# Attention and mixture-of-experts block on one core: the router's small tables first, gate bias rows ahead of the table matmuls, one up bias load sooner

## The chip, the cores and the metric

The kernel runs on 1 core of one Trainium2 chip. The metric is the device time of one execution in microseconds (us), the median over several runs. Lower is better.

## The reference

The input x is [1, 64, 32, 256]. The layer is an axial attention with a pair bias, added to x, and after it a mixture of experts over 2048 tokens of width 256, added again. What matters here is the second half:

```python
logits = x @ router_w + router_b                 # 2048 x 8
probs = jax.nn.softmax(logits, axis=-1)
top_v, top_i = jax.lax.top_k(probs, TOP_K)       # TOP_K = 2
top_v = top_v / jnp.sum(top_v, axis=-1, keepdims=True)
weights = jnp.zeros((T, E)).at[jnp.arange(T)[:, None], top_i].set(top_v)
gate = jnp.einsum('td,edi->eti', x, gate_w) + gate_b[:, None, :]
up = jnp.einsum('td,edi->eti', x, up_w) + up_b[:, None, :]
h = jax.nn.silu(gate) * up
expert_out = jnp.einsum('eti,eid->etd', h, down_w) + down_b[:, None, :]
y = jnp.einsum('te,etd->td', weights, expert_out)
```

There x is the normalised token, and all of it is float32. There are 8 experts with 512 hidden columns each.

## The kernel before

**Stages.** The kernel first normalises x and stacks it by token. Then a loop of 8 steps does the attention of 32 columns each; beside it the weights of one expert per step are loaded and split into a float16 high and low part (ScalarE and GpSimd). Then comes the router, and then 39 blocks of 128 token slots, each belonging to one expert: gather the tokens from DRAM, gate and up matmul, silu, product, down matmul, scale, and add into the output with an indirect DMA. The order of work on every engine is written out by hand, and semaphores tie the engines together. Each of them runs its own list strictly in order, so a waiting instruction holds back all that stands behind it.

**The router.** Of the names in the views, att_t, kq, z_two, gate, w_stage and att_n are buffers of the attention that the router uses again. Its steps:

- GpSimd makes thirteen tables. Three of them are large or belong to the output: `r_number` (L489, an iota of 128x1024), its float16 copy `r_count` (L490), and zeros in `ws_flat` (L492), which two DMAs (L494) write to the output's pad rows. These are 256 rows behind the 2048 real ones, into which empty slots scatter. The other ten are small (L497 to L508): `before`, the triangle for counting tokens; iotas for tiles, thresholds, token numbers and experts (`r_rev`); and masks. Every table increments route_p. The order of GpSimd's list is: last weight split (L467), the large iota and copy, zeros and pad DMAs, the ten small tables, four normalised tiles of tokens (L513), then the second half of the softmax (L517 to L526).
- VectorE takes the statistics of all tokens (L1426, L1429), their reciprocal roots (L1201 to L1204, behind a square root of ScalarE) and the negated mean (L1432), which releases rs_ready. Then it waits for all thirteen tables, copies `r_rev` to float32 (L1436), and goes on from the logits (L1442) through the two largest of eight, the mark of both, the running count (L1458), slots (L1465 to L1484), and `r_values` and `r_place` (L1487 to L1498). `r_count` is read there for the first time. At L1508 it makes the gather indices.
- ScalarE copies transposed tokens, normalises twelve tiles (L1098) after rs_ready, takes one exponential (L1115), and then copies the gate bias of each expert from PSUM to SBUF (L1123), after the output rows of `x_rows` have been stored.
- TensorE transposes the logits (L810), spreads each expert's gate bias row over 128 partitions (L818, `gate_bias_rows`: one matmul with 8 partitions for one expert, shown as two in the trace), does the counting matmuls (L824 to L826), 32 matmuls that put token numbers into slots (L833, "table matmuls"), and warming matmuls (L571, `keep_warm`) that compute nothing needed. `GATE_BANK` says which of the eight PSUM banks takes which expert's bias row; the seventh and eighth row (e of 6 or more) reuse banks 0 and 1 and wait until ScalarE has emptied them.
- SyncE issues the transfers: token rows to DRAM in four DMAs (`token_rows`, L368), then the routing weights next to them (L373), whose elements are 32 bytes. GpSimd's first gather (L541) waits for all of these, for the pads, for the output rows, and for L1508.

**Loads in the attention loop.** SyncE's list is, for each step j, the value placement of step j+1 (L338, four DMAs), a copy of tokens (L326), and the three weight loads of expert j+1 (L309). In `load_weights` four loads of the up bias are slipped in (`spread_up_biases`, L292), 512 KB each over 128 partitions. They go into the stacked tokens, and therefore wait until the token copies have landed (z_in0, z_in1). Three stand in the loads of the seventh expert (e is 6) and the fourth behind the gate load of the eighth.

```python
                    if e == EXPERTS - 2 or (e == EXPERTS - 1 and k == 0):
                        for i in range(2):
                            sp.wait_ge(s[f"z_in{i}"], 16 * (PAIRS // 2 - 1))
                        spread_up_biases(k if e == EXPERTS - 2 else 3)
```

Of the kernel before, what the change touches and what calls it, by code (L numbers as in the profile page):

```python
# [7 lines left out]
L_COL = 256  # L8
# [3 lines left out]
EXPERTS = 8  # L12
FF = 512
P = 128
# [13 lines left out]
TOKENS = D_MODEL * N_SEQ  # L28
TILES = TOKENS // P
TOP_K = 2  # L30
SLOT = P
# [8 lines left out]
PIECE = ASSIGN // PIECES  # L40
GATE_BANK = (0, 1, 2, 5, 6, 7, 0, 1)
# [6 lines left out]
def build(nc, x, pairs, ln_m_g, ln_m_b, ln_p_g, ln_p_b, Wq, Wk, Wv, Wg, bg, Wb, Wo, bo,  # L48
# [5 lines left out]
    with ctx:  # L54
# [48 lines left out]
        bank = [banks[:, i, :] for i in range(8)]  # L103
# [45 lines left out]
        N_TABLES = 13  # L149
        N_CONST, N_PAR, N_CENTER, N_ONES, N_PREP = 10, 18, 7, 3, 1 + 1 + 1 + 1 + 2  # L150
# [57 lines left out]
        rev_f = att_t[:, 328:336]  # L208
# [61 lines left out]
        def _(sp):  # L270
# [28 lines left out]
            def load_weights(e):  # L299

                parts = (gate_w[e].rearrange("(c p) i -> p c i", p=P), up_w[e].rearrange("(c p) i -> p c i", p=P),
                         down_w[e].rearrange("(c p) l -> p c l", p=P))
                for k in range(3):
                    if e >= 1:
                        if k < 2:
                            sp.wait_ge(s["w_hi_done"], 2 * (e - 1) + k + 1)
                        sp.wait_ge(s["w_lo_done"], 3 * (e - 1) + k + 1)
                    c = 2 if k < 2 else 4
                    sp.dma_start(w_stage[:, k, :].rearrange("p (c i) -> p c i", c=c),  # L309
                                 parts[k]).then_inc(s[f"w_in{k}"], 16)  # L310
                    if e == EXPERTS - 3 and k >= 1:
                        sp.wait_ge(s["x1_ready"], 1 + PAIRS // 2)
                        rows_to_out(0, k - 1)
                    if e == EXPERTS - 2 or (e == EXPERTS - 1 and k == 0):
                        for i in range(2):
                            sp.wait_ge(s[f"z_in{i}"], 16 * (PAIRS // 2 - 1))
                        spread_up_biases(k if e == EXPERTS - 2 else 3)
# [74 lines left out]
        def _(pool):  # L392
# [91 lines left out]
            def table(ins):  # L484
                ins.then_inc(s["route_p"], 1)
                n_r[0] += 1
                pool.wait_ge(s["route_p"], n_r[0])
            pool.wait_ge(s["w_lo_done"], 3 * EXPERTS)
            table(pool.iota(r_number, pattern=[[1, P], [0, PIECE]], base=0, channel_multiplier=0))  # L489
            table(pool.tensor_copy(r_count, r_number))  # L490
            pool.wait_ge(s["x1_ready"], 1 + PAIRS)
            table(pool.memset(ws_flat[:, 0:L_COL], 0.0))  # L492
            for i in range(2):
                pool.dma_start(out[TOKENS + SLOT * i:TOKENS + SLOT * (i + 1), :], ws_flat[:, 0:L_COL])\  # L494
                    .then_inc(s[f"y_landed{i}"], 16)

# [12 lines left out]
            assert n_r[0] == N_TABLES  # L509

            pool.wait_ge(s["rs_ready"], 1)
            for n in range(TILES - 4, TILES):
                pool.tensor_scalar(xn[:, n, :], x_rows[:, n, :], mv[:, n, 0:1], rs_col[:, n:n + 1],  # L513
                                   ALU.subtract, ALU.mult).then_inc(s["xn_pool"], 1)

# [50 lines left out]
        def _(pe):  # L566
# [255 lines left out]
            gate_bias_rows(range(3))  # L822
# [5 lines left out]
            gate_bias_rows(range(3, 6))  # L828
# [7 lines left out]
            gate_bias_rows(range(6, EXPERTS))  # L836
            keep_warm(3, bank[3])
# [352 lines left out]
        def _(dve):  # L1190
# [239 lines left out]
            dve.wait_ge(s["mean_ready"], 2 * TILES)  # L1430
            rsqrt(4, rs_col, mv[:, :, 1], EPS_TOK, sd_col, tmp_col, None)
            dve.scalar_tensor_tensor(out=neg_mean, in0=mv[:, :, 0], scalar=-1.0, in1=rs_col,  # L1432
                                     op0=ALU.mult, op1=ALU.mult).then_inc(s["rs_ready"], 1)

            dve.wait_ge(s["route_p"], N_TABLES)
            step(dve.tensor_copy(rev_f, r_rev))  # L1436
# [49 lines left out]
            values = r_values.rearrange("p t (c a) -> p t c a", c=PIECES)  # L1486
            step(dve.tensor_tensor(values, r_count[:, 0:BLOCKS, :].unsqueeze(2).broadcast_to(by_block),  # L1487
# [164 lines left out]
```

## Time and profile before

| what | value |
|---|---|
| median of 3 runs | 350.35 us |
| lowest and highest | 348.79 and 351.41 us |
| the profiled execution's own time | 347.03 us |
| its span | 345.2 us |
| TensorE, VectorE, ScalarE, GpSimd busy | 283.2, 273.9, 195.2, 209.1 us |
| mean granted TensorE clock | 0.926 |

The profile is of one execution. Its span is what the profiler saw between first and last instruction. Shares of busy time are averages over stages: TensorE's 82% of the span is 100% in the blocks and far less in the router. A row of a timeline has start, duration, engine, line, operation and, in brackets, the idle time before it with what ended it. PE is TensorE, DVE VectorE, ACT ScalarE, POOL GpSimd, SP SyncE; an engine's name with q is its instruction queue. The granted clock is 1.00 at 2.4 GHz and 0.50 at 1.2 GHz.

### The profile page before, as it was taken

What the parts mean: (1) busy time and instruction counts of PE and PEld (TensorE: products, weight loads), DVE (VectorE), ACT (ScalarE), POOL (GpSimd) and SP (SyncE); (2) the same over time, 40 slices, a digit from 0 to 9 for tenths busy, and PEclk for the clock granted to TensorE, in tenths of its full rate; (3) what the DMA queues carried; (4) which work ended last, traced back from release to release, by engine and by line L of the source; (5) the groups of instructions that cost most, each with busy time, mean ns of one, the idle gap of its engine ahead of it and who ended that gap; (6) DMA issues with size and microseconds to landing.
All of it is one profiled execution on the core that took longest, in us unless ns stands there. A gap on an engine that the chain in (4) does not pass through costs nothing.

```text
span 345.2 us, 11090 instructions
## 1 busy us (share of the span) xinstructions
PE 283.2 (82%) x3762; PEld 176.0 (51%) x3763; DVE 273.9 (79%) x568; ACT 195.2 (57%) x357; POOL 209.1 (61%) x171
## 2 busy tenths in 40 slices
PE   0496857868877768918989999999999999999970
PEld 0186434535554446404346666666666666666640
DVE  3998786979999998879578888778787888888840
ACT  0268676958779756494245555555555555555430
POOL 2633042777888987861523666685848676776461
PEclk9998995899999987955599999999999999999996
DMA  7550111455868999646235977877777786977552
GB/s 181 96 173 14 64 36 29 133 193 158 238 223 234 279 313 329 171 102 148 70 76 77 142 125 122 144 129 123 125 128 130 124 141 118 144 134 122 94 78 30
DMA packets 72288, 47.36 MB, mean 137 GB/s; under 512 B 48536, under 2 KB 63896, under 8 KB 72128
## 3 DMA queue, kind: packets, MB, share of 16 engines
q1 hardware_dynamic: 63904, 36.19, 41.5%
q0 software_dynamic: 7584, 10.65, 20.1%
q8 instruction: 15, 0.25, 0.3%
q10 hardware_dynamic: 768, 0.14, 0.3%
q14 instruction: 17, 0.14, 0.2%
HBM read 23.43 MB, written 9.63 MB: 96 GB/s over the span
## 4 chain that ended last, share of the span: by engine, by line
PE 44%; DVE 18%; issue 12%; DMA 10%; POOL 7%; ACT 5%; POOLq 2%; ACTq 0%; DVEq 0%; SPq 0%
PE bank L871 22%; PE bank L894 10%; DMA out_dram<-z_two,gate 7%; DVE maxes L1333 4%; DVE s_exp L1342 3%; PE bank L607 2%; DVE e_t L1352 2%; PE bank L859 2%; POOL w_exp L456 2%; PE bank L571 2%; DMA w_stage<-in_L_ffn_up_w_dram 2%; ACT kq L1044 2%; DMA w_exp<-in_L_conv_pairs_dram 2%; PE bank L698 1%; POOLq L548 1%
## 5 line engine op out<-in xcount | busy, mean ns | idle before, releaser
L871 PE MATMUL bank<-w_exp,v_t 128*128 x468 | 114.1, 381 | 1.6 <-DVE v_t L1534 1.6
L553 POOL DMA_INDIRECT out_dram<-z_two,gate x39 | 67.4, 1729 | 50.3 <-ACT z_two L1167 27.6
L871 PEld LDWEIGHTS bank<-w_exp,v_t 128*128 128x128 f16 x468 | 45.9, 98 | 41.9 <-issue 3.9
L894 PE MATMUL bank<-w_exp,kq 128*128 x468 | 57.7, 273 | 0.8 <-DVE w_stage L1580 0.8
L541 POOL DMA_INDIRECT w_stage<-token_rows,gate x39 | 41.1, 1053 | 22.3 <-issue 7.9
L894 PEld LDWEIGHTS bank<-w_exp,kq 128*128 128x128 f16 x468 | 45.5, 98 | 14.8 <-issue 1.3
L1158 ACT ACTIVATE kq<-w_stage 128x512 f16<-128x512 f32 x38 | 23.9, 630 | 38.0 <-DVE w_stage L1563 38.0
L456 POOL TENSOR_TENSOR w_exp<-w_stage,w_exp 128x1024 f16<-128x1024 f32 x16 | 34.2, 2136 | 18.0 <-ACT w_exp L1055 18.0
L1570 DVE TENSOR_TENSOR kq<-w_stage,kq 128x512 f16<-128x512 f32 x38 | 26.3, 692 | 16.7 <-ACT kq L1158 16.7
L1555 DVE TENSOR_TENSOR kq<-bank,z_stack 128x512 f32<-128x512 f32 x39 | 27.0, 691 | 7.9 <-PE bank L871 7.8
L1563 DVE TENSOR_TENSOR w_stage<-s_exp,kq 128x512 f32<-128x512 f32 x39 | 27.2, 697 | 4.7 <-DVE kq L1555 1.8
L1131 ACT ACTIVATE v_t<-bank 128x256 f16<-128x256 f32 x39 | 14.9, 382 | 22.7 <-PE bank L859 22.1
L1144 ACT ACTIVATE s_exp<-s_exp 128x512 f32<-128x512 f32 x39 | 24.5, 628 | 5.3 <-DVE s_exp L1550 5.0
L1550 DVE TENSOR_TENSOR s_exp<-bank,x_rows 128x512 f32<-128x512 f32 x39 | 26.6, 683 | 0.0
L1352 DVE STREAM_TRANSPOSE e_t<-s_exp 128x1024 f32<-128x1024 f32 x16 | 19.8, 1240 | 4.5 <-ACT s_exp L1050 4.5
L1044 ACT ACTIVATE kq<-bank,kb_head,head_mask 128x512 f32<-128x512 f32 x32 | 22.2, 781 | 0.0
L1333 DVE TENSOR_REDUCE maxes<-bank 128x32 f32<-128x1024 f32 x16 | 19.5, 1216 | 3.3 <-PE bank L698 3.3
L1167 ACT ACTIVATE z_two<-w_stage,gate 128x256 f32<-128x256 f32 x39 | 19.3, 494 | 4.9 <-DMA out_dram<-z_two,gate 3.7
L1050 ACT ACTIVATE s_exp<-s_exp 128x1024 f32<-128x1024 f32 x16 | 16.9, 1055 | 8.4 <-DVE s_exp L1342 8.2
L571 PE MATMUL bank<-ones_h,ident_h 128*128 128x512 f16 x29 | 10.2, 513 | 13.4 <-DVE small L1204 13.4
L1342 DVE TENSOR_TENSOR s_exp<-bank,maxes 128x1024 f32<-128x1024 f32 x16 | 19.3, 1204 | 0.3
L1534 DVE TENSOR_TENSOR v_t<-bank,v_t 128x256 f16<-128x256 f32 x39 | 16.2, 415 | 3.7 <-ACT v_t L1131 3.7
(251 smaller groups left out, 493.0 us busy)
## 6 DMA issues: line engine op xcount, KB each, us to landing
w_stage<-in_L_ffn_gate_w_dram SPq DMA_DIRECT2D x8, 512.0 KB, 3.9
w_stage<-in_L_ffn_up_w_dram SPq DMA_DIRECT2D x8, 512.0 KB, 4.9
w_stage<-in_L_ffn_down_w_dram SPq DMA_DIRECT2D x8, 512.0 KB
v_t<-v_row SPq DMA_DIRECT2D x32, 72.0 KB, 2.3
x_rows<-in_x_dram SPq DMA_DIRECT2D x8, 256.0 KB, 6.3
out_dram<-x_rows SPq DMA_DIRECT2D x4, 512.0 KB, 6.0
z_stack<-in_L_ffn_up_b_dram SPq DMA_DIRECT2D x4, 512.0 KB, 7.1
token_rows<-v_t SPq DMA_DIRECT2D x4, 512.0 KB, 6.1
```

What stands on the lines that cost most here:

```text
L456: pool.tensor_tensor(lo, w_stage[:, k, :], hi, ALU.subtract).then_inc(s["w_lo_done"], 1)
L541: pool.indirect_dma_start(xg[b % 4], None, token_rows, bass.IndirectOffsetOnAxis(t_gather[:, b:b + 1], 0))\
L553: pool.indirect_dma_start(out, bass.IndirectOffsetOnAxis(t_scatter[:, b:b + 1], 0), yw[b % 2], None, compute_op=ALU.add).then_inc(s[f"y_la ...
L871: mm = pe.matmul(GU[par][k][:], xs[par][:, c, :], w_exp[:, w * W_EXP + k * W_PIECE + c * FF:][:, bass.ds(e, FF)], start=(n == 0), stop=(n ...
L894: mm = pe.matmul(YB[:, 0:L_COL], hs[par][:, c, :], w_exp[:, w * W_EXP + 2 * W_PIECE + c * L_COL:][:, bass.ds(e, L_COL)], start=(n == 0), s ...
L1044: act.activation(k_exp[:, h, :], bank[5 if j else 1], ACT.Identity, bias=kb_head[:, h:h + 1], scale=head_mask[:, h:h + 1]).then_inc(s["k_r ...
L1333: dve.tensor_reduce(maxes[:, c, :], banks[:, 2 * c:2 * c + 2, :].rearrange("p g (a m) -> p (g a) m", m=N_SEQ), AX.X, ALU.max).then_inc(s[" ...
L1342: dve.tensor_tensor(s_exp[:, c, :, :].rearrange(rows, m=N_SEQ), banks[:, 2 * c:2 * c + 2, :].rearrange(rows, m=N_SEQ), maxes[:, c, :].unsq ...
L1352: dve.transpose(e_t[:, c, :, :].rearrange("p g t -> p (g t)"), s_exp[:, c, :, :].rearrange("p g t -> p (g t)")).then_inc(s["et_ready"], 1)
L1550: dve.tensor_tensor(g_sum[par], bank[2 * par][:], gate_b_all[:, bass.ds(e * FF, FF)], ALU.add)\
L1555: dve.tensor_tensor(u_sum[par], bank[2 * par + 1][:], up_b_all[:, bass.ds(e * FF, FF)], ALU.add)\
L1563: dve.tensor_tensor(h_sb[par], g_silu[par], u_sum[par], ALU.mult).then_inc(s["h_ready"], 1)
```

## The change

It moves instructions and changes no arithmetic.

- GpSimd: the ten small tables come first, then the large iota and its copy, then the four normalised tiles, and the zeros with the two pad DMAs last. VectorE waits for the ten (`N_SMALL`) before its copy of `r_rev`, and that copy moves ahead of the reciprocal roots; for the large table it waits where it first reads it.
- TensorE: five gate bias rows instead of three ahead of the counting matmuls, the other three behind those and ahead of the table matmuls, none behind the table matmuls. There, seven warming matmuls instead of three. Experts 4 and 5 exchange their banks 6 and 7.
- SyncE: the fourth up bias load moves from behind the gate load of the eighth expert to behind that of the sixth (e is 5).

```diff
-GATE_BANK = (0, 1, 2, 5, 6, 7, 0, 1)
+GATE_BANK = (0, 1, 2, 5, 7, 6, 0, 1)
...
+        N_SMALL = N_TABLES - 3
...
-                    if e == EXPERTS - 2 or (e == EXPERTS - 1 and k == 0):
+                    if e == EXPERTS - 2 or (e == EXPERTS - 3 and k == 0):
...
             pool.wait_ge(s["w_lo_done"], 3 * EXPERTS)
-            table(pool.iota(r_number, pattern=[[1, P], [0, PIECE]], base=0, channel_multiplier=0))
-            table(pool.tensor_copy(r_count, r_number))
             pool.wait_ge(s["x1_ready"], 1 + PAIRS)
-            table(pool.memset(ws_flat[:, 0:L_COL], 0.0))
-            for i in range(2):
-                pool.dma_start(out[TOKENS + SLOT * i:TOKENS + SLOT * (i + 1), :], ws_flat[:, 0:L_COL])\
-                    .then_inc(s[f"y_landed{i}"], 16)
-
             table(pool.memset(before, 0.0))
...
             table(pool.memset(r_one8, 1.0))
-            assert n_r[0] == N_TABLES
-
+            assert n_r[0] == N_SMALL
+            table(pool.iota(r_number, pattern=[[1, P], [0, PIECE]], base=0, channel_multiplier=0))
+            table(pool.tensor_copy(r_count, r_number))
             pool.wait_ge(s["rs_ready"], 1)
             for n in range(TILES - 4, TILES):
                 pool.tensor_scalar(xn[:, n, :], x_rows[:, n, :], mv[:, n, 0:1], rs_col[:, n:n + 1],
                                    ALU.subtract, ALU.mult).then_inc(s["xn_pool"], 1)
+
+            table(pool.memset(ws_flat[:, 0:L_COL], 0.0))
+            assert n_r[0] == N_TABLES
+            for i in range(2):
+                pool.dma_start(out[TOKENS + SLOT * i:TOKENS + SLOT * (i + 1), :], ws_flat[:, 0:L_COL])\
+                    .then_inc(s[f"y_landed{i}"], 16)
...
-            gate_bias_rows(range(3))
+            gate_bias_rows(range(5))
             pe.wait_ge(s["sel_ready"], 1)
...
-            gate_bias_rows(range(3, 6))
+            gate_bias_rows(range(5, EXPERTS))
             pe.wait_ge(s["values_ready"], 1)
...
-            gate_bias_rows(range(6, EXPERTS))
-            keep_warm(3, bank[3])
+            keep_warm(7, bank[3])
...
             dve.wait_ge(s["mean_ready"], 2 * TILES)
+            dve.wait_ge(s["route_p"], N_SMALL)
+            step(dve.tensor_copy(rev_f, r_rev))
             rsqrt(4, rs_col, mv[:, :, 1], EPS_TOK, sd_col, tmp_col, None)
...
-
-            dve.wait_ge(s["route_p"], N_TABLES)
-            step(dve.tensor_copy(rev_f, r_rev))
...
+            dve.wait_ge(s["route_p"], N_SMALL + 2)
             step(dve.tensor_tensor(values, r_count[:, 0:BLOCKS, :].unsqueeze(2).broadcast_to(by_block),
```

GpSimd behind the last weight split, before: w_stage holds first the large table (L489, L490), then the zeros (L492).

```order
L489 IOTA w_stage 128x1024
L490 CAST w_stage<-w_stage 128x1024
L492 MEMSET w_stage 128x256
L494 DMA out_dram<-w_stage 128x256 x2
L497 MEMSET z_two 128x128
L498 AFFINE_SELECT z_two<-z_two 128x128
L500 IOTA att_t 128x128
L501 IOTA att_t 128x16
L503 IOTA att_t 64x16 x2
L505 IOTA att_t 128x8
L506 MEMSET kq 128x128
L507 MEMSET kq 128x8
```

And now, from the last of the small tables' iotas on (the tables from the memset of z_two to this iota stand ahead of it, right behind the weight split):

```order
L499 IOTA att_t 128x8
L500 MEMSET kq 128x128
L501 MEMSET kq 128x8
L502 MEMSET kq 128x8
L504 IOTA w_stage 128x1024
L505 CAST w_stage<-w_stage 128x1024
L508 TENSOR_SCALAR v_t<-x_rows,small 128x256 x4
L511 MEMSET w_stage 128x256
L514 DMA out_dram<-w_stage 128x256 x2
L518 TENSOR_SCALAR kq<-kq 128x16
```

The large table went behind the small ones, and the zeros and pad DMAs behind the normalised tiles (L508), right ahead of the softmax denominator (L518).

VectorE at the token statistics, before: the cast to att_t is the copy of r_rev, and the instruction behind it makes the logits.

```order
L1429 BN_AGGR small<-g_pre 128x2 x16
L1201 RECIPROCAL small<-small 128x16
L1202 SCALAR_TENSOR_TENSOR small<-small 128x16
L1203 SCALAR_TENSOR_TENSOR small<-small 128x16
L1204 SCALAR_TENSOR_TENSOR small<-small 128x16
L1432 SCALAR_TENSOR_TENSOR g_pre<-small 128x16
L1436 CAST att_t<-att_t 128x8
L1442 TENSOR_TENSOR att_n<-bank,small 128x128
```

And now:

```order
L1429 BN_AGGR small<-g_pre 128x2 x16
L1432 CAST att_t<-att_t 128x8
L1201 RECIPROCAL small<-small 128x16
L1202 SCALAR_TENSOR_TENSOR small<-small 128x16
L1203 SCALAR_TENSOR_TENSOR small<-small 128x16
L1204 SCALAR_TENSOR_TENSOR small<-small 128x16
L1434 SCALAR_TENSOR_TENSOR g_pre<-small 128x16
L1441 TENSOR_TENSOR att_n<-bank,small 128x128
```

The cast and its wait went ahead of the reciprocal.

TensorE from the transposed logits to the warming matmuls, before; v_row holds the gate bias rows:

```order
L810 MATMUL bank<-ident,v_t 128x128 x4
L818 MATMUL bank<-v_row,ident 128x512 x3
L824 MATMUL bank<-kq,ones_h 128x8
L825 MATMUL bank<-kq,z_two 128x128
L826 MATMUL bank<-kq,ones_h 128x128
L818 MATMUL bank<-v_row,ident 128x512 x3
L833 MATMUL bank<-gate,s_exp 128x39 x32
L818 MATMUL bank<-v_row,ident 128x512 x2
L571 MATMUL bank<-ones_h,ident_h 128x512 x3
```

And now:

```order
L811 MATMUL bank<-ident,v_t 128x128 x4
L819 MATMUL bank<-v_row,ident 128x512 x5
L825 MATMUL bank<-kq,ones_h 128x8
L826 MATMUL bank<-kq,z_two 128x128
L827 MATMUL bank<-kq,ones_h 128x128
L819 MATMUL bank<-v_row,ident 128x512 x3
L834 MATMUL bank<-gate,s_exp 128x39 x32
L572 MATMUL bank<-ones_h,ident_h 128x512 x7
```

Two bias rows went from behind the table matmuls to ahead of the counting matmuls, and the three behind the counts are now experts 5, 6 and 7.

## Rows read from the trace of the kernel before

**Rows 1.** Windows: length, busy us (instructions) of PE, PEld, DVE, ACT, POOL; PEclk, DMA share, GB/s.

```profile
148.00:170.00 22.00, 14.71 (x52) 6.53 (x52) 19.23 (x59) 11.85 (x22) 10.75 (x13) 0.50 0.48 117
170.00:178.00 8.00, 6.49 (x29) 3.07 (x29) 4.25 (x8) 2.93 (x8) 2.82 (x3) 0.91 0.27 65
178.00:288.00 110.00, 110.00 (x692) 69.09 (x693) 89.56 (x161) 59.07 (x134) 70.02 (x50) 1.00 0.76 124
```

**Rows 2.** Chain that ended last, 140 to 172 us: start us, us, what.

```profile
140.73 1.41 POOL w_stage L489
...
147.68 0.11 POOL kq L508
...
161.04 2.49 PE bank L833 x32
163.53 3.71 PE bank L818 x4
167.24 1.39 PE bank L571 x3
...
170.15 2.10 PE bank L871 x6
```

**Rows 3.** Timeline of VectorE, router stage: start us, us, then idle before and releaser.

```profile
145.01 0.25 DVE L1201 RECIPROCAL small<-small 128x16 f32<-128x16 f32 x1 [0.44 <-ACT small L1110]
...
145.93 0.17 DVE L1432 SCALAR_TENSOR_TENSOR g_pre<-small 128x16 f32<-128x16 f32 x1
147.81 0.17 DVE L1436 CAST att_t<-att_t 128x8 f32<-128x8 int32 x1 [1.71 <-POOL kq L508]
...
156.07 0.25 DVE L1476 RECIPROCAL kq<-kq 128x16 f32<-128x16 f32 x1
...
163.64 0.20 DVE L1508 TENSOR_SCALAR gate<-bank 128x39 int32<-128x39 f32 x1 [0.19 <-PE bank L833]
```

**Rows 4.** Timeline of GpSimd, router stage.

```profile
143.94 1.41 POOL L494 DMA_DIRECT2D out_dram<-w_stage  x2 [0.33 <-POOL w_stage L492]
...
147.90 4.90 POOL L513 TENSOR_SCALAR v_t<-x_rows,small 128x256 f32<-128x256 f32 x4
154.50 0.27 POOL L517 TENSOR_SCALAR kq<-kq 128x16 f32<-128x16 f32 x1 [1.71 <-ACT kq L1115]
...
164.74 1.11 POOL L541 DMA_INDIRECT w_stage<-token_rows,gate  x1 [6.38 <-DVE gate L1508]
```

**Rows 5.** SyncE's last small write to token_rows: its issue, and its time to landing.

```profile
159.00 1.08 SPq L373 DMA_DIRECT2D token_rows<-w_stage  x1
...
token_rows<-w_stage SPq DMA_DIRECT2D x1, 32.0 KB, 3.6
```

**Rows 6.** DMA queues, 154 to 158 us: packets, MB, share of 16 engines.

```profile
q1 hardware_dynamic: 1072, 1.06, 99.1%
```

**Rows 7.** Timeline of ScalarE, router stage.

```profile
152.16 1.28 ACT L1115 ACT_TABLE_LOAD   x1
154.20 0.22 ACT L1115 ACTIVATE kq<-kq 128x16 f32<-128x16 f32 x1 [0.76 <-DVE kq L1460]
...
155.84 2.04 ACT L1123 ACTIVATE x_rows<-bank 128x512 f32<-128x512 f32 x4
```

**Rows 8.** Timeline of TensorE, gate bias rows.

```profile
144.13 2.84 PE L818 MATMUL bank<-v_row,ident 8*128 8x512 f32 x6
...
154.51 5.48 PE L818 MATMUL bank<-v_row,ident 8*128 8x512 f32 x6
```

**Rows 9.** DMA queues, 145 to 147 us.

```profile
q0 software_dynamic: 96, 0.26, 37.2%
```

**Rows 10.** Value placement of the seventh step: last issue, its time to landing, its first reader.

```profile
116.00 0.59 SPq L338 DMA_DIRECT2D v_t<-v_row  x1
...
v_t<-v_row SPq DMA_DIRECT2D x1, 72.0 KB, 2.2
...
119.42 0.76 PE L714 MATMUL bank<-v_t,e_t 128*32 128x36 f32 x64 [0.25 <-DVE e_t L1352]
```

## The prediction

> **What bounds the kernel now.** I read the windows of busy time first, since they tell which stage has which limit. From 178 to 288 us TensorE is busy for 110.00 of 110.00 us at granted clock 1.00 [rows 1]: the expert blocks run at TensorE's pace, so whatever moves the first expert matmul moves the end by as much, and nothing in this change touches a block. Before it lies the router, and there the chain of waits is the view to follow. It runs on GpSimd through L489 (140.73) to L508, whose 0.11 us end at 147.79 [rows 2], and only then does VectorE go on: L1436 stands at 147.81 after 1.71 us of idle time put down to L508 [rows 3]. From there the chain is VectorE's small steps, then TensorE: 32 table matmuls from 161.04 to 163.53, four passes of gate bias rows (3.71 us), three warming matmuls (1.39 us) to 168.63, the first token transposes and, at 170.15, the first expert matmul [rows 2].
>
> The third view is what runs beside the chain. The gathers of token rows need the bookkeeping of L1508 (ends 163.84) [rows 3] and also the landing of everything written to token_rows; the first gather starts at 164.74 [rows 4], 0.90 after L1508. The last small write is issued at 159.00 and takes 3.6 us to land, 162.6 [rows 5]. So today that landing is 1.2 us early, but the DMA engines were 99.1% busy from 154 to 158 [rows 6].
>
> **The change, part by part.** The profiled execution took 347.03 us (span 345.2 and 1.8 around it). The runs' median is 350.35, 3.3 above; I work a difference on the former and subtract it from the latter.
>
> *GpSimd's order.* The ten small tables take 147.79 − 145.35 (end of the pad issues, 143.94 + 1.41 [rows 4]) = 2.44 us. Begun at 140.73 they end at 143.2. VectorE's aggregates end at 145.01 − 0.44 = 144.57 [rows 3], so its new wait for ten tables is already met by 1.4 us. Its moved cast (0.17 us) sits in the 0.44 us in which it waits for ScalarE's root anyway: cost nothing, and 0.2 if that root came sooner. The router's first multiply follows L1432 (ends 146.10) instead of L1436 (147.98): 1.71 of idle plus the cast and a handoff, **1.9 us** sooner on VectorE.
>
> The large iota and its cast now follow. Old GpSimd took from 140.73 to 143.94 for these two and the memset, so they are done by 143.2 + 3.2 = 146.4 at the latest, against 146.10 when L513 can start. L513 (4.90 us) began at 147.90 and now ends by 151.3 [rows 4]; the memset and two pad issues (1.41 and some 0.3 + 0.3) end at 153.3. What is queued behind them is L517, which VectorE's L1476 waits for. ScalarE's table load still ends at 152.16 + 1.28 = 153.44, since its twelve normalisations did not move, and the exponential (0.22) [rows 7] gives L517 its data at 153.7, just after GpSimd is free; L517 ends at 154.0. L1476 stood at 156.07, now 154.2. Cover 0.2 us: the two edits meet almost at once.
>
> The Trainium skill speaks against exactly this move. The two old pad issues took 1.41 us together while VectorE worked through its statistics [rows 4]. SBUF — State Buffer, section "SBUF: two separate sides", says that GpSimd cannot write a DMA's descriptors while VectorE holds the port pair that both share. By the row the sum keeps 1.4 us for the issues; by the rule they could stretch over VectorE's router steps, the last rival below.
>
> *Bias rows on TensorE.* Six passes took 2.84 us at the fast clock (0.47 each) and 5.48 us at the slow one (0.91) [rows 8]. Five experts are ten passes: 144.13 to 148.9, in time that was idle: the next rows began at 154.51 [rows 8], right behind the router's counts, now 152.6. Three experts then stand ahead of the table matmuls. The first takes until 154.5. The next needs a bank that ScalarE empties: exponential over at 153.7, then what took 154.42 to 155.84, then 0.51 a copy [rows 7], thus 155.6. Two experts at 1.82 each end at 159.2, and the table matmuls can start at 161.04 − 1.9 = 159.1. Cost 0.1, or nothing at the fast clock. This is the new tight spot.
>
> Behind the table matmuls (end 161.6) 3.71 us of bias rows are gone and four warming matmuls are added: 7 x 0.46 = 3.2, so TensorE is ready at 164.9 instead of 168.6. What is late next is the data.
>
> *The pads among the row writes.* Around 145–147 us the software queue used 37.2% of 2 us on sixteen engines [rows 9], 0.74 us of all of them, in a lull. Now it comes at about 153, in the 99.1% stretch. The small writes are issued 1.9 sooner but stand behind it all: they land between 162.6 − 1.9 = 160.7 (nothing delays them) and 162.6 + 0.74 = 163.3. I take 163.3, the row of a full stretch being the nearest. The gather then starts 0.9 later, at 164.2. From its start to arrival is at least its own 1.11 us and at most 168.6 − 164.74 = 3.9; I take 3.2, nearer to the 3.6 of a small write. Transposes at 167.4 instead of 168.6: **1.2 us** is what the path gets out of the 1.9 and 3.7.
>
> *The clock.* The granted clock was 0.50 from 148 to 170 and averaged 0.91 over 170–178 [rows 1], so 1.4 us of that were at 1.2 GHz: the first 1.3 us of expert matmuls, costing half, 0.65. Before them TensorE had worked with almost no gap since 161.04. Now it stops at 164.9 for 2.5 us. Seven warming matmuls without a break may raise the clock sooner (gain up to 0.65), the pause may make it rise later. I take 0.
>
> *The up bias load.* Moved to the sixth expert's load, it adds 512 KB at about 107.5 us and waits for a copy that has just been issued. The stretch of [rows 6] moved 1.06 MB in 4 us, so it costs at most 2.0 us of the DMA engines. First in line behind it are the value placements: the last was issued at 116.00, landed 2.2 later at 118.2, and is wanted by L714 at 119.42 [rows 10], 1.2 us of cover. Loss 0 to 0.8; I take 0, since weight loads come faster than that stretch. At the end of the loop the last up weights come sooner, but VectorE sets that stage: 0.
>
> Sum: −1.2. Profiled, 345.8; against the median, **349.1**.
>
> **The rivals.** *The row writes do not gate* (25%). If the pads slip in without delaying the small writes, the gather follows L1508: 162.85, data at 166.05, TensorE ready at 164.9. Gain 2.6, with the fast clock 3.2: 347.1 to 347.8, say 347.5. For it: the landing is 1.2 us early today. Against: 99.1%.
>
> *The clock stays low* (13%), which ends slower. The pause from 164.9 to 167.4 is where it happens. Its price is half of each microsecond that expert matmuls run at 1.2 GHz beyond today's 1.3; it decides from 3.7 us on, when 2.4 x 0.5 eats the 1.2. At 6.5 us it costs 2.6: 350.35 + 1.4 = 351.8. For it: 22 us at 0.50 in which TensorE was busy most of the time. Against: full-width warming matmuls are what stood before today's rise, and there are more of them.
>
> *The up bias load hurts attention* (12%). The placements land 0.8 after they are wanted, the step slips once: gain 0.4, 349.9.
>
> *GpSimd is late for L517, or the pads delay the row writes by more than their own 0.74* (8%). L1476, and the small writes after it, come 1 to 1.5 us later than in my sum: gain 0 to 0.2, 350.3. The Trainium skill's rule above would act here; its own measured stretch of a descriptor write, from 620 to 3100 ns, would put each issue near 3 us, and no row here shows such a one.
>
> **How the numbers follow.** My case has 42%, and 0.65 either way for the clock. A measurement of this kernel tells about 1%, 3.5 us, from no change. Nearly every case lies within that: faster by more needs the first rival with the fast clock and some luck of runs whose spread is 348.79 to 351.41. Faster 0.14, within 1% 0.80, slower 0.06. The range takes the first rival's best less part of that spread at one end (346.4) and the slower rival at the other (351.7).
>
> **What would show it.** VectorE's cast straight after the aggregates with no 1.71 us wait; its L1508 counterpart ending near 161.9; the pad issues after L513 and software-queue traffic near 153–155; the small writes landing at 163, the first gather at 164.2 rather than 162.85; TensorE idle before its transposes near 167.4; the first expert matmul near 168.9. Wrong, if TensorE arrives there last, if a table matmul waits for bias rows by more than 0.2, if L1476 waits, or if the blocks no longer keep 110 of 110 us busy.

## The result, and the profile after

The changed kernel took 350.69 us (median of 20 runs, 348.61 to 351.99) against 348.79 (20 runs, 347.28 to 351.87). The ratio is 1.0053 with a 95% interval of 1.0034 to 1.0072. It is slower, by some 1.9 us, where 1.2 us less was forecast. The size is within the predicted 1%, the sign is not. The 350.35 that the forecast of 349.1 was taken from was a median of 3 runs, 1.6 above that of these 20. So the two times are 1.6 apart, while the change that was forecast and the one that was measured are 3.1 apart. The profiled execution took 351.16 us (span 349.3).

The windows of busy time, columns as in [rows 1]:

```profile
148.00:170.00 22.00, 18.23 (x58) 7.10 (x56) 19.28 (x64) 13.11 (x25) 10.42 (x15) 0.52 0.49 115
170.00:178.00 8.00, 6.76 (x22) 3.00 (x23) 1.88 (x5) 1.71 (x5) 4.20 (x5) 0.61 0.31 82
178.00:288.00 110.00, 108.59 (x677) 67.38 (x676) 89.57 (x160) 58.01 (x133) 66.72 (x50) 1.00 0.71 122
```

The last row still shows expert blocks at TensorE's pace. The middle row is the news: the granted clock over 170 to 178 us is 0.61, where it was 0.91. The two rows are not of the same work, though: before, the first expert matmul stood at 170.15, right at the window's start, and now it stands at 172.78.

The chain that ended last (start us, us, what):

```profile
117.41 0.59 SPq L339
118.05 3.10 DMA v_t<-v_row
121.19 0.77 PE bank L715 x53
...
159.67 1.99 SPq L374
161.71 5.44 DMA token_rows<-w_stage
...
168.08 2.89 DMA w_stage<-token_rows,gate
171.01 0.70 PE bank L859 x2
...
172.78 2.74 PE bank L871 x6
```

Two transfers are on it that were not before: a value placement (v_row to v_t) in the attention loop, and the last small write to token_rows. In [rows 2] the chain ran through GpSimd's tables and then through TensorE's bias rows instead.

VectorE's timeline. The first row is the end of the token aggregates, from which the stages below are counted, since everything before it shifts from one execution to the next:

```profile
146.47 1.29 DVE L1429 BATCH_NORM_AGGREGATE small<-g_pre 128x2 f32<-128x12 f32 x16
147.80 0.41 DVE L1432 CAST att_t<-att_t 128x8 f32<-128x8 int32 x1
...
149.16 0.17 DVE L1434 SCALAR_TENSOR_TENSOR g_pre<-small 128x16 f32<-128x16 f32 x1
149.25 0.28 DVE L1441 TENSOR_TENSOR att_n<-bank,small 128x128 f32<-128x128 f32 x1
...
157.36 0.25 DVE L1475 RECIPROCAL kq<-kq 128x16 f32<-128x16 f32 x1 [0.26 <-POOL kq L518]
...
165.29 0.20 DVE L1508 TENSOR_SCALAR gate<-bank 128x39 int32<-128x39 f32 x1 [0.54 <-PE bank L834]
```

The 1.71 us wait of [rows 3] is gone. From the end of the aggregates (147.76) to the index conversion L1508 it is now 17.53 us; before, 163.64 − 144.57 = 19.07.

GpSimd's timeline (against [rows 4]):

```profile
149.52 4.98 POOL L508 TENSOR_SCALAR v_t<-x_rows,small 128x256 f32<-128x256 f32 x4 [1.34 <-DVE g_pre L1434]
155.08 1.43 POOL L514 DMA_DIRECT2D out_dram<-w_stage  x2 [0.33 <-POOL w_stage L511]
157.00 0.26 POOL L518 TENSOR_SCALAR kq<-kq 128x16 f32<-128x16 f32 x1 [0.50 <-ACT kq L1115]
...
168.08 1.10 POOL L542 DMA_INDIRECT w_stage<-token_rows,gate  x1 [8.43 <-DMA token_rows<-w_stage]
```

What released the gather has changed: in [rows 4] L1508 on VectorE, now the landing of the small write. SyncE's row for the two small writes, and the last one's time to landing (against [rows 5]):

```profile
159.67 4.23 SPq L374 DMA_DIRECT2D token_rows<-w_stage  x2
...
token_rows<-w_stage SPq DMA_DIRECT2D x1, 32.0 KB, 5.4
```

TensorE's timeline (against [rows 8] and the end of [rows 2]):

```profile
147.32 7.27 PE L819 MATMUL bank<-v_row,ident 8*128 8x512 f32 x10
...
158.96 3.78 PE L819 MATMUL bank<-v_row,ident 8*128 8x512 f32 x4 [1.30 <-ACT x_rows L1123]
162.66 2.51 PE L834 MATMUL bank<-gate,s_exp 128*128 128x39 f16 x32
165.00 3.17 PE L572 MATMUL bank<-ones_h,ident_h 128*128 128x512 f16 x7
171.01 0.69 PE L859 MATMUL bank<-ident,w_stage 128*128 128x128 f32 x2 [2.84 <-DMA w_stage<-token_rows,gate]
...
172.78 2.74 PE L871 MATMUL bank<-w_exp,v_t 128*128 x6 [0.23 <-DVE v_t L1534]
```

TensorE is idle for 2.84 us ahead of its transposes, and the first six expert matmuls take 2.74 us, which is the price at 1.2 GHz. The granted clock is the last but two of the numbers in these windows:

```profile
165.00:168.00 3.00, 3.00 (x10) 0.86 (x8) 2.50 (x8) 0.00 (x0) 0.00 (x0) 0.50 0.14 9
...
176.00:178.00 2.00, 2.00 (x10) 0.86 (x9) 1.32 (x3) 1.11 (x3) 0.90 (x1) 0.92 0.05 8
```

So the seven warming matmuls end at the low clock. It rises at about 176.3, 3.5 us after the first expert matmul; before, by the same windows, it rose 1.3 us after it.

The attention step of [rows 10], and the one behind it:

```profile
121.19 0.77 PE L715 MATMUL bank<-v_t,e_t 128*32 128x36 f32 x64 [0.92 <-DMA v_t<-v_row]
...
133.50 1.19 PE L715 MATMUL bank<-v_t,e_t 128*32 128x36 f32 x64 [1.67 <-issue]
```

The first one waited 0.25 for VectorE before; now it waits 0.92 for the placement. It comes 6.62 us after the value matmuls that close the sixth step, and came 5.96 after them before.

### The profile page after: what moved, and what is told of

It reads as the page before. It is cut to its first block, busy times and chain, and to the rows that moved or that the text cites. A ratio compares the mean times of both kernels' runs of the same rounds, so it can differ in the third digit from the quotient of the medians.

```text
span 349.3 us, 11099 instructions
## 1 busy us (share of the span) xinstructions
PE 288.0 (82%) x3766; PEld 177.4 (51%) x3767; DVE 274.5 (79%) x568; ACT 194.9 (56%) x357; POOL 208.3 (60%) x171
## 4 chain that ended last, share of the span: by engine, by line
PE 45%; DVE 16%; DMA 11%; issue 11%; ACT 7%; POOLq 2%; POOL 2%; SPq 2%; ACTq 0%; DVEq 0%
PE bank L871 20%; PE bank L894 9%; DMA out_dram<-z_two,gate 5%; PE bank L699 3%; DVE maxes L1333 3%; PE bank L608 2%; ACT kq L1044 2%; DVE s_exp L1342 2%; PE bank L690 2%; PE bank L859 2%; POOLq L549 2%; ACT v_t L1098 2%; PE bank L715 2%; DMA token_rows<-w_stage 2%; DMA kq<-kq 2%
## 5 line engine op out<-in xcount | busy, mean ns | idle before, releaser
L554 POOL DMA_INDIRECT out_dram<-z_two,gate x39 | 66.1, 1695 | 51.6 <-ACT z_two L1167 33.4
L572 PE MATMUL bank<-ones_h,ident_h 128*128 128x512 f16 x33 | 12.3, 539 | 13.3 <-DVE small L1204 13.3
L715 PE MATMUL bank<-v_t,e_t 128*32 128x36 f32 x1024 | 14.0, 210 | 9.0 <-DVE e_t L1352 4.1
```

The costliest lines, as they stand in the source:

```text
L554: pool.indirect_dma_start(out, bass.IndirectOffsetOnAxis(t_scatter[:, b:b + 1], 0), yw[b % 2], None, compute_op=ALU.add).then_inc(s[f"y_la ...
```

## The experiments

All kernels compute the whole reference; where the count of warming matmuls differs, nothing but warming is added. Each ratio is to the kernel before, run beside it on the same chip, with its 95% interval. "Bridged" means that warming matmuls are added to fill TensorE's pause before the token transposes.

**The up bias load alone** (before, with one line of the change):

```diff
-                    if e == EXPERTS - 2 or (e == EXPERTS - 1 and k == 0):
+                    if e == EXPERTS - 2 or (e == EXPERTS - 3 and k == 0):
```

> The kernel before with only the up bias load moved to the sixth expert's loads. Theory Q (the load lengthens the DMA backlog, and the value placements of the last two attention steps land after TensorE wants them): slower than before by 1.5 to 2.5 us, the last placement landing 6 to 7 us after its issue instead of 5.7, TensorE idle over 1 us ahead of the eighth step's first value matmuls, the token aggregates about 2 us later relative to the first step. Theory R (the router's new order is what costs, the load is free): same as before within 0.4 us, and no such idle time.

Measured: 1.0044 (1.0016 to 1.0072), 351.48 against 349.66. TensorE's timeline of the two attention steps:

```profile
119.96 0.77 PE L714 MATMUL bank<-v_t,e_t 128*32 128x36 f32 x64 [0.81 <-DMA v_t<-v_row]
...
132.01 1.19 PE L714 MATMUL bank<-v_t,e_t 128*32 128x36 f32 x64 [1.41 <-issue]
```

The load costs some 1.5 us by itself: a part of the change that the prediction put at nothing. SyncE's four placement issues for the seventh step show where it starts, in the kernel before and then in this one:

```profile
112.65 3.94 SPq L338 DMA_DIRECT2D v_t<-v_row  x4
```

```profile
112.63 5.47 SPq L338 DMA_DIRECT2D v_t<-v_row  x4
```

They begin at the same time and take 1.5 us longer to issue, while the last of them lands 2.4 after its issue, 2.2 before. The last placement of the eighth step lands 6.5 after its issue, as expected, but that tells nothing: with the loads in their old places it takes from 5.3 to 7.2.

**The change without that load** (the same line turned back):

```diff
-                    if e == EXPERTS - 2 or (e == EXPERTS - 3 and k == 0):
+                    if e == EXPERTS - 2 or (e == EXPERTS - 1 and k == 0):
```

> The changed kernel with the up bias load back in its old place. Q: about 2 us faster than the changed kernel, hence between 0.5 us faster and 0.5 us slower than before, since the router gains 1.5 us up to the gather indices and gives it back at the landing of the small writes and to the clock. R: as slow as the changed kernel, 1.5 to 2 us above before.

Measured: 1.0015 (0.9983 to 1.0048). The wait for the placement is gone (0.25, on VectorE), and the rest of the change gains nothing either: the first gather starts 20.67 after the aggregates (before 20.17), and TensorE pauses 3.08 us. The time lies at the upper end of what was expected.

**And the pads early** (on the kernel above: zeros and pad DMAs right behind the ten small tables, the large table behind the normalised tiles; the late zeros and pad DMAs go, and VectorE waits for all tables where it reads the large one):

```diff
-            table(pool.iota(r_number, pattern=[[1, P], [0, PIECE]], base=0, channel_multiplier=0))
-            table(pool.tensor_copy(r_count, r_number))
+            table(pool.memset(ws_flat[:, 0:L_COL], 0.0))
+            for i in range(2):
+                pool.dma_start(out[TOKENS + SLOT * i:TOKENS + SLOT * (i + 1), :], ws_flat[:, 0:L_COL])\
+                    .then_inc(s[f"y_landed{i}"], 16)
             pool.wait_ge(s["rs_ready"], 1)
...
+            table(pool.iota(r_number, pattern=[[1, P], [0, PIECE]], base=0, channel_multiplier=0))
+            table(pool.tensor_copy(r_count, r_number))
```

> As the last one, and the zeros and pad writes stand right behind the ten small tables, the large iota and its copy behind the four normalised tiles. Theory P (the pad writes among the row writes hold up the small writes, which now release the first gather): the first gather starts 1 to 1.5 us sooner after the token aggregates than with the pads late (20.3 us in the changed kernel, so about 19), and the time falls by 0.8 to 1.5 us against the kernel before. Rival (the row writes alone keep the queue full until then): the gather starts within 0.3 us of the late pads' version and the time is the same as that.

Measured: 1.0002 (0.9973 to 1.0031). The gather comes 19.18 after the aggregates, 1.0 sooner than before the change, and the pause shrinks to 1.75. The ratio does not show this gain of 0.8 to 1.5 us that was expected; its interval is wide enough to hide most of it.

**TensorE's part alone** (before, with the bias rows, banks and warming of the change):

```diff
-            gate_bias_rows(range(3))
+            gate_bias_rows(range(5))
...
-            gate_bias_rows(range(3, 6))
+            gate_bias_rows(range(5, EXPERTS))
...
-            gate_bias_rows(range(6, EXPERTS))
-            keep_warm(3, bank[3])
+            keep_warm(7, bank[3])
```

> The kernel before with only TensorE's part of the change: five bias rows early, three ahead of the table matmuls, seven warming matmuls behind. Theory G (what TensorE gains it loses to waiting for the gather and to the clock): first gather at the same time, TensorE idle 0.5 to 1.5 us before the first token transposes, time 0.7 us faster to 0.5 us slower. Rival (TensorE's arrival set the first block, nothing else): 0.7 to 1.2 us faster.

Measured: 1.0054 (1.0028 to 1.0081), 1.9 us slower, outside both expectations. Windows of 2 us:

```profile
168.00:170.00 2.00, 0.78 (x4) 0.10 (x1) 1.79 (x6) 0.00 (x0) 1.59 (x2) 0.98 0.22 68
170.00:172.00 2.00, 0.87 (x4) 0.36 (x4) 1.49 (x7) 0.57 (x2) 1.50 (x2) 0.88 0.36 85
172.00:174.00 2.00, 1.06 (x3) 0.51 (x4) 0.42 (x1) 0.02 (x1) 1.34 (x2) 0.50 0.43 118
174.00:176.00 2.00, 2.00 (x7) 1.00 (x6) 0.00 (x0) 0.00 (x0) 0.00 (x0) 0.50 0.30 68
176.00:178.00 2.00, 2.00 (x6) 0.66 (x5) 1.02 (x2) 0.97 (x3) 0.73 (x1) 0.50 0.00 0
```

The clock had risen when the warming matmuls ended (0.98). TensorE was then busy for 0.78 and 0.87 us of two windows, with 1.63 us without a matmul ahead of the transposes and 1.66 ahead of the expert matmuls; the clock fell again, and the first expert matmuls, from 172.94, ran at 1.2 GHz.

**The same, bridged** (14 warming matmuls for 7):

```diff
-            keep_warm(7, bank[3])
+            keep_warm(14, bank[3])
```

> The kernel before with TensorE's part of the change, and fourteen warming matmuls behind the table matmuls instead of seven. Theory K (what TensorE's part costs is the clock: the pause before the first token transposes leaves the first expert matmuls at 1.2 GHz for longer): the pause shrinks from over 1.6 us to under 0.5, the third group of six expert matmuls starts 5.0 to 5.3 us after the first and not 6 to 7, and 1.3 to 2 us of the 1.9 come back, so the time is that of before within 0.6 us. Rival L (the cost lies in the bias rows ahead of the table matmuls or elsewhere): the time stays 1.5 us or more above before.

Measured: 1.0006 (0.9977 to 1.0034). Its windows:

```profile
168.00:170.00 2.00, 2.00 (x9) 0.82 (x8) 1.83 (x6) 0.00 (x0) 1.60 (x2) 0.75 0.05 11
170.00:172.00 2.00, 1.87 (x9) 0.66 (x7) 1.76 (x9) 0.38 (x1) 1.42 (x2) 1.00 0.42 125
172.00:174.00 2.00, 0.49 (x3) 0.33 (x4) 0.66 (x2) 0.20 (x1) 1.67 (x2) 1.00 0.40 99
```

and TensorE's timeline of the first expert matmuls, this kernel's, then that of the one without the bridge:

```profile
173.51 1.47 PE L870 MATMUL bank<-w_exp,v_t 128*128 x6 [1.64 <-DVE v_t L1533]
175.03 2.75 PE L870 MATMUL bank<-w_exp,v_t 128*128 x12
177.84 1.46 PE L870 MATMUL bank<-w_exp,v_t 128*128 x6
```

```profile
172.94 2.74 PE L870 MATMUL bank<-w_exp,v_t 128*128 x6 [1.66 <-DVE v_t L1533]
175.90 3.96 PE L870 MATMUL bank<-w_exp,v_t 128*128 x12
179.91 1.46 PE L870 MATMUL bank<-w_exp,v_t 128*128 x6
```

From the start of the first group of six to that of the last it is 4.33 with the bridge and 6.97 without: 2.6 us of clock, by the profile; the two ratios differ by 0.5%, 1.7 us. The 1.64 us without a matmul ahead of the first group stand in the bridged kernel too, and the clock held through them. Moving the bias rows in itself gains and costs nothing that this interval shows, since nothing behind them was ready sooner.

**GpSimd's and VectorE's part alone, pads late as in the change** (before, with the order of the tables and the two waits; of the lines that move only the new places are shown):

```diff
+            table(pool.memset(ws_flat[:, 0:L_COL], 0.0))
+            assert n_r[0] == N_TABLES
+            for i in range(2):
+                pool.dma_start(out[TOKENS + SLOT * i:TOKENS + SLOT * (i + 1), :], ws_flat[:, 0:L_COL])\
+                    .then_inc(s[f"y_landed{i}"], 16)
...
+            dve.wait_ge(s["route_p"], N_SMALL)
+            step(dve.tensor_copy(rev_f, r_rev))
             rsqrt(4, rs_col, mv[:, :, 1], EPS_TOK, sd_col, tmp_col, None)
```

> The kernel before with only GpSimd's new order and VectorE's moved wait, pad writes late as in the change, bias rows and up bias load as before. If the parts add up (all but the load +0.5, TensorE's part +1.9), it is 1.0 to 1.8 us faster than before; first gather released by the small writes 19.3 to 20.3 us after the aggregates, TensorE arriving there without a pause of over 1 us. Rival (the small writes' landing takes all of the gain by itself): same as before within 0.5 us.

Measured: 1.0027 (0.9998 to 1.0057), a clear miss. **The same with the pads early** (the edit of the third kernel):

> As the last one, with the pad writes right behind the ten small tables and the large iota behind the normalised tiles. Theory P (pad writes among the row writes delay the small writes): first gather about 19.2 us after the aggregates, 0.7 to 1.2 sooner than with late pads; TensorE's bias rows and warming fill the time until then, so that nothing is paid to the clock: 1.5 to 2.3 us faster than before. Rival: no faster than the version with late pads.

Measured: 0.9966 (0.9935 to 0.9997), 1.2 us faster where 1.5 to 2.3 were expected. Part of the expectation failed: there is no pause ahead of the transposes, but three warming matmuls left the clock low, and the first six expert matmuls took 2.74 us. SyncE's small writes and GpSimd's first gather, in the first of the two and then in the second:

```profile
157.76 4.25 SPq L374 DMA_DIRECT2D token_rows<-w_stage  x2
...
166.20 1.10 POOL L542 DMA_INDIRECT w_stage<-token_rows,gate  x1 [8.46 <-DMA token_rows<-w_stage]
```

```profile
158.63 3.12 SPq L374 DMA_DIRECT2D token_rows<-w_stage  x2
...
165.75 1.10 POOL L541 DMA_INDIRECT w_stage<-token_rows,gate  x1 [7.15 <-DMA token_rows<-w_stage]
```

The aggregates ended at 145.18 and 146.60, so the gather comes 21.02 and 19.15 after them: late pads cost the gather 1.9 us and the kernel 0.6%, 2.1 us.

**Everything that helped, bridged** (the third kernel with 12 warming matmuls for 7):

```diff
-            keep_warm(7, bank[3])
+            keep_warm(12, bank[3])
```

> GpSimd's order with early pads, TensorE's new bias rows, and twelve warming matmuls instead of seven; up bias load as before. K: the pause ahead of the first transposes is under 0.5 us, the expert matmuls reach 2.4 GHz at most 1.3 us after the first, 1.5 to 2.3 us faster than before. L: same as before, like the version with seven.

Measured: 0.9924 (0.9893 to 0.9956), 346.06 against 348.80: 2.7 us, more than was expected. No pause is left before the transposes, and the expert matmuls start at 2.4 GHz. Run again on another chip:

> The kernel with early pads, the new bias rows and twelve warming matmuls once more, as the comparison for the next ones on the same chip. If its gain was no accident of the first runs: 1.5 to 3.5 us faster than before.

0.9922 (0.9893 to 0.9952).

**The load moved sooner on this kernel** (the line of the first experiment):

> The first one of these with the up bias load moved to the sixth expert's loads, as in the change. Q: 1.0 to 2.0 us slower than it, from a later landing of the last value placements. Rival: the same within 0.4 us.

Measured: 0.9972 (0.9938 to 1.0005), beside 0.9922 without it on the same chip: 1.7 us. TensorE, the two attention steps:

```profile
123.31 0.78 PE L714 MATMUL bank<-v_t,e_t 128*32 128x36 f32 x64 [1.22 <-DMA v_t<-v_row]
...
135.45 1.19 PE L714 MATMUL bank<-v_t,e_t 128*32 128x36 f32 x64 [2.19 <-issue]
```

**A load moved later instead** (two of the four behind the seventh expert's, two behind the eighth's):

```diff
-                    if e == EXPERTS - 2 or (e == EXPERTS - 1 and k == 0):
+                    if e >= EXPERTS - 2 and k < 2:
...
-                        spread_up_biases(k if e == EXPERTS - 2 else 3)
+                        spread_up_biases(k if e == EXPERTS - 2 else 2 + k)
```

> The last one with the third up bias load moved the other way, from the down load of the seventh expert to the gate load of the eighth, the fourth behind the up load of the eighth. Theory Q (what stands in the DMA queue ahead of the last value placement sets TensorE's start in the eighth step): the last placement lands 1 to 2 us sooner after its issue, TensorE's wait ahead of the eighth step's value matmuls falls from 0.8 to 2.5 us to under 0.5, and the time falls by 0.5 to 1.5 us against the same kernel without this. Rival (VectorE sets the pace of that step whatever the placement does): no wait of TensorE there, and the same time within 0.4 us.

Measured: 0.9871 (0.9827 to 0.9914), 345.51 us in 6 runs: the fastest kernel of the case, though its interval overlaps that of the kernel it is built on. The last placement lands 5.0 us after its issue, and neither step waits for one:

```profile
120.02 0.76 PE L714 MATMUL bank<-v_t,e_t 128*32 128x36 f32 x64 [0.26 <-DVE e_t L1351]
...
130.81 1.19 PE L714 MATMUL bank<-v_t,e_t 128*32 128x36 f32 x64
```

In the second profile of the kernel that it is built on the last placement took 5.3 (6.7 in the first), and the eighth step's first value matmuls came at 131.19 without a wait as well. So the profiles don't show what gained the time, if it was gained.

**The changed kernel, only bridged** (14 for 7):

> The changed kernel with fourteen warming matmuls instead of seven. Theory K (part of its loss is the pause and the clock): no pause before the first transposes, third group of six expert matmuls 5.0 to 5.5 us after the first instead of 6.1, 0.5 to 1.5 us faster than the changed kernel, so 0.4 to 1.4 us above before. Rival: as slow as the changed kernel, 1.9 us above before.

Measured: 1.0019 (0.9989 to 1.0048), where the changed kernel has 1.0053. The first and third groups of expert matmuls are 4.33 apart again (6.06 in the changed kernel), with 1.16 us of pause left ahead of the transposes, where none was expected; the seventh attention step still waits 1.06 for its placement.

**All of them in one table.** Router: from the end of the aggregates to the third group of six expert matmuls, which holds both the path and its clock, less the 30.54 us (175.11 − 144.57) of the kernel before. Load: 1.7 where it was moved sooner, from the pair of timings on one chip above. The end of the aggregates bears it out, counted from the last value matmuls of the sixth step: 32.5 to 33.8 us in the four profiles with the moved load, 31.1 to 32.4 in the nine with it in its place, 1.5 apart on average. Sum is the two together, and measured is (ratio − 1) x 349.

```
kernel                        router  load   sum   measured
changed                         +0.5  +1.7  +2.2   +1.9
load alone                      -0.1  +1.7  +1.6   +1.5
changed, load back              -0.2    0   -0.2   +0.5
  and pads early                -1.5    0   -1.5   +0.1
  and bridged (two chips)       -2.6    0   -2.6   -2.7, -2.7
    and load sooner             -2.6  +1.7  -0.9   -1.0
TensorE's part alone            +2.4    0   +2.4   +1.9
  bridged                        0.0    0    0.0   +0.2
router order, pads late         +1.6    0   +1.6   +0.9
router order, pads early        -0.9    0   -0.9   -1.2
changed, bridged                -1.3  +1.7  +0.4   +0.7
```

Eleven of the twelve timings here lie within 0.7 us of the sum; the one that doesn't is the kernel with early pads and no bridge, off by 1.6, and for that there is no explanation here: its first expert matmuls ran partly at the low clock, as the router column already counts. Its profile is of a quick execution, 347.76 against a median of 350.01. The agreement of the others is weaker than it looks. The interval of each ratio is about 1 us either way, the load's 1.7 was taken from the row "and load sooner", which so agrees by construction, and each router number is one profile, which leaves out the blocks: from the third group to the last down matmuls they took 158.57 us in the kernel before, the shortest of all, 159.70 in the odd one and 160.44 in the one with the load sooner. The kernel with a load moved later is left out, since its load column isn't known.

## Why the prediction was wrong

**The up bias load: the step that failed.** I bounded it by 0 to 0.8 and took 0, "since weight loads come faster than that stretch", with 1.2 us of cover from one landing in [rows 10]. Four kernels with the moved load show a wait of 0.81 to 1.22 us for the placement in the seventh step; none of the others has one. In those four SyncE needs 4.87 to 5.74 us to issue the seventh step's four placements, in the other ten 3.77 to 4.77, and from the first issue to the last landing it is 7.3 to 7.7 against 5.5 to 6.3. I had looked at the landing of one placement and left out that its issue could come later. The bound on the wait itself held: the seventh step's first value matmuls came 0.6 to 1.0 later. What was not in the sum is that this isn't all: by the end of the aggregates it is 1.5 on average, and the times say 1.5 and 1.7 in two pairs that differ in this load alone (1.3 between the changed kernel and the one with the load back). Where the rest arises is not shown. The wait of the eighth step ("issue" in the rows) proves nothing by itself: with the load in its place it came out anywhere from none to 2.61 us.

**The profile before was an early one.** Its aggregates end at 144.57, and the nine profiles with the load in its place lie between there and 147.47. In these nine the cover in the seventh step runs from 0.2 to 1.2 us. The 1.2 of [rows 10] and the 0.23 us of waiting in the eighth step were at the good end, so that I reasoned from a margin that most of the profiles don't have.

**VectorE's gain: right.** I had 1.9 us; the logits step stands 1.49 after the aggregates (149.25 − 147.76), where in the trace of before it stood 3.45 after them. The new wait costs nothing, as said; the cast took 0.41, not 0.17. Up to L1508 1.54 us are left. The rest went where the prediction saw the tight spots: 0.26 of waiting at L1475, where "the two edits meet almost at once", and 0.54 at L1508 (0.19 before), whose table matmuls now stand behind bias rows that had waited 1.30 for ScalarE. I had costed these at 0 and 0.1.

**The pads among the row writes: right in direction, too small.** I let them delay the small writes' landing by 0.74 of transfer, to 19.6 between aggregates and gather. It was 20.3, 0.15 later than before, so the gather gave back all of the 1.5. What grew was the issuing on SyncE, from 1.70 us for two small writes to 4.23, and then their landing, from 3.6 to 5.4. With pads early they are 3.12 and 5.0. In two pairs the late pads made the gather 1.5 and 1.9 later (20.67 against 19.18, 21.02 against 19.15), so they are the larger part of what was lost. With early pads the gather still waits for the small writes, some 0.6 longer than the indices of L1508 would make it; I put this down to their coming sooner behind 2 MB of row writes, which no run tests by itself. The Trainium skill, DMA: Bandwidth & Descriptors, section "Queues, rings and completion order", says that a DMA's semaphore write lands only after all earlier writes of that DMA engine, across its queues. The landing behind another queue's 256 KB agrees with it, though by no more than 5.4 against 5.0, and no run here tells the rule from plain sharing of the engines; the longer issue is not in that rule.

**The clock: right place, wrong choice.** I named the pause (164.9 to 167.4) and had the slower case at 13%, "from 3.7 us on". Counted from the aggregates, TensorE was ready at 20.4 after them, against 20.3 in my sum, and the first expert matmul came 25.0 after them, 0.56 sooner than before instead of 1.2. Then 1.1 us were lost to the clock: the third group of six stands 6.06 behind the first instead of 4.96. I took 0 because I gave a pause and more warming the same weight. Seven warming matmuls did not raise the clock here at all, so that in the changed kernel nothing fell in the pause: the clock only rose later, 3.5 us after the first expert matmul instead of 1.3, and half of these 2.2 is the 1.1. In two other kernels (TensorE's part alone, and the change without its load) it had risen during warming, to 1.00 over 169 to 170, and was at 0.50 again before the first expert matmul. In every bridged kernel it rose during warming and held. But bridging does two things at once, more warming and a shorter pause ahead of the transposes (1.16 us at most), and the runs don't part them. The pause alone is not the cause: the kernel before and the router order with early pads have none, only three warming matmuls, and began their expert matmuls at the low clock too (2.10 and 2.74 for the first six). Six expert matmuls took 2.74 us at 1.2 GHz and 1.47 at 2.4. The Trainium skill, TensorE: Matmul & The Clock Gate, section "HAM oscillation — how this bites in real kernels", puts the penalty at half of the time spent at the low clock; the trace agrees, with 1.1 us lost to 2.2 more at the low clock.

**The sum again.** Put what was measured in place of the three terms: −1.2, and 0.6 for the later gather, 1.1 for the clock, 1.7 for the load make +2.2, against 1.9 measured.

**The rivals.** The likeliest one, that the row writes do not gate, is out: the gather waits for them in every kernel with the new order. "The pads delay the row writes by more" (8%), "the clock stays low" (13%) and "the load hurts attention" (12%) all happened at once; I had priced each as if the others did not, and the gain they had to be set against was only 1.2 us. The skill's rule on descriptors that I set against the sum did not show: the two pad issues took 1.43 us beside VectorE's router steps, 1.41 before. The skill's 620 and 3100 ns are times of a whole transfer; I had used them for an issue.

## What to carry to other kernels

A warming burst has to last nearly until the work that it is for: where an edit makes TensorE ready sooner than its data, try a longer one. Here five to seven more warming matmuls brought back 1.2 to 2.7 us in three pairs of kernels. A transfer that is moved sooner can be paid by the small transfers behind it, in their issue as well as in their landing, and a cover read from one landing of one profile is not a cover. A store that nobody waits for still belongs where the queues are quiet: 256 KB of zeros among the row writes cost 2.1 us, more than the 1.2 that the reordering gained without them there.

## What the hardware did that I had not expected

- Issuing two DMAs of 32 KB took SyncE 1.70 us before and 4.23 in the changed kernel, for the same two transfers. With the pads early it was 3.12, so what else the queues hold has a part in it; how the issue comes to be stretched no run here shows.
- Five experts' bias rows kept TensorE busy for 7.27 us, but in the whole stretch from 148 to 170 us, with 18.2 of 22 us busy, the granted clock was 0.52. With TensorE's part alone it reached 0.98 over 168 to 170, behind the warming, and was back at 0.50 at the first expert matmul, after 1.63 and 1.66 us without a matmul on either side of the transposes. With the first of the two pauses filled it stayed at 1.00 through the second, 1.64 us.
